# Keys and values of all batches made between two layers, and the fill-in chunks of a turn laid out anew

## What is computed

```python
# layer 0: x += tanh(g)*mix(ctx, norm(x)); x += tanh(g)*moe64(norm(x))    (64 experts, top 8)
# layer 1, attention: 16 heads of 16, causal, keys and values from ctx_512 (4, 256, 64)
qp = norm(x) @ Wq.T
k, v = split(ctx_512 @ Wkv_expand.T)          # do not depend on x
scores = einsum(q, k) / 4, causal mask; attn = softmax(scores)
x = x + tanh(g_xattn[1]) * (attn @ v) @ Wout.T
# layer 1, experts: 8 routed (top 2) + shared (2 more chunks), all computed for all tokens
x1, x3 = silu(xf @ w_gate), xf @ w_up         # 10 chunks of 128 hidden units
x = x + tanh(g_ffn[1]) * sum_c comb_c * (x1*x3)_c @ w_down_c
```

## Time and profile before

| | us |
|---|---|
| median of 3 runs (612.03 to 613.97) | 612.97 |
| the profiled execution's own time | 607.06 |
| span of that execution, first to last instruction | 605.3 |
| PE busy in the span | 425.7 (70%) |
| DVE busy | 346.5 (57%) |
| ACT busy | 184.0 (30%) |
| POOL busy | 146.3 (24%) |
| mean granted TensorE clock | 0.834 of full |

### The profile page before, as it was taken

How to read it: one execution, slowest core, us unless ns; L and a number is a source line. 1 busy time by engine, 2 the same in 40 slices (tenths; PEclk the granted TensorE clock), 3 DMA queues, 4 the chain that set the end, 5 groups by cost and what they waited for, 6 DMA issues and landing times.

```text
span 605.3 us, 9222 instructions
## 1 busy us (share of the span) xinstructions
PE 425.7 (70%) x2738; PEld 355.7 (59%) x2738; DVE 346.5 (57%) x1050; ACT 184.0 (30%) x377; POOL 146.3 (24%) x154
## 2 busy tenths in 40 slices
PE   5065553302999999997136637899699978999686
PEld 3043342202998889885025425787488856887586
DVE  2978875396344444443367803487547883681554
ACT  3212210100333333343611412525252342517231
POOL 1306675673000000002775370001710000000000
PEclk9976565555999999997557756999779996999899
DMA  7996222266699999993332130000310000000000
GB/s 272 427 410 264 88 96 79 78 238 211 209 301 322 324 312 326 377 396 128 100 91 67 38 104 0 1 2 16 100 44 0 2 0 0 18 2 2 2 17 18
DMA packets 36693, 82.96 MB, mean 137 GB/s; under 512 B 6000, under 2 KB 16048, under 8 KB 34864
## 3 DMA queue, kind: packets, MB, share of 16 engines
q1 hardware_dynamic: 22800, 55.83, 26.3%
q0 software_dynamic: 6144, 16.79, 8.6%
q10 hardware_dynamic: 7712, 9.90, 4.6%
HBM read 50.44 MB, written 31.92 MB: 136 GB/s over the span
## 4 chain that ended last, share of the span: by engine, by line
PE 52%; DVE 15%; issue 12%; ACT 7%; POOL 6%; another core or an unknown queue 4%; DMA 2%; SPq 1%; DVEq 0%; POOLq 0%; ACTq 0%
PE PS L555 11%; PE PS L565 7%; POOL slots_in L432 5%; PE PS L644 4%; PE PS L618 4%; PE PS L542 3%; PE PS L764 2%; PE PS L657 2%; PE PS L712 2%; PE PS L659 2%; PE PS L658 2%; DVE TH L1312 2%; DVE WORK L1049 2%; DVE TOP L1045 2%
## 5 line engine op out<-in xcount | busy, mean ns | idle before, releaser
L442 POOL DMA_INDIRECT GB<-slots_out,IDXG x64 | 68.4, 1069 | 214.9 <-SPq L365 139.7
L555 PE MATMUL PS<-XTE,WR 128*128 128x128 f32 (+2 forms) x512 | 79.7, 299 | 0.0
L432 POOL DMA_INDIRECT slots_in<-XNA,IDX x64 | 64.9, 1014 | 36.8 <-issue 27.6
L555 PEld LDWEIGHTS PS<-XTE,WR 128*128 128x128 f32 x512 | 70.2, 193 | 0.6 <-ACT XTE L854 0.4
L1234 DVE TENSOR_TENSOR HE<-SGE,PS 128x128 f32<-128x128 f32 (+2 forms) x64 | 20.0, 312 | 62.9 <-ACT SGE L863 60.0
L565 PE MATMUL PS<-WR,HE 128*80 128x256 f32 (+2 forms) x198 | 53.6, 381 | 0.3 <-DVE HE L1234 0.3
L657 PE MATMUL PS<-XH,WGH 128*128 128x256 f32 x160 | 49.7, 311 | 0.3 <-DVE XL L1430 0.3
L854 ACT COPY XTE<-PS 128x256 f32<-128x256 f32 (+2 forms) x64 | 26.3, 410 | 74.5 <-PE PS L542 70.6
L644 PE MATMUL PS<-WD,XW 128*128 128x256 f32 x160 | 41.8, 384 | 7.0 <-DVE XW L1319 3.5
L542 PE MATMUL PS<-CF,XE 80*128 80x80 f32 (+2 forms) x198 | 28.3, 256 | 25.7 <-DMA XE<-slots_in 25.7
L658 PE MATMUL PS<-XL,WGH 128*128 128x256 f32 x160 | 45.3, 283 | 0.0
(11 more groups left out here) (226 smaller groups left out, 843.2 us busy)
## 6 DMA issues: line engine op xcount, KB each, us to landing
WR<-in_wexp SPq DMA_DIRECT2D x64, 384.0 KB, 5.0
slots_in<-GB SPq DMA_DIRECT2D x12, 1024.0 KB, 18.7
XE<-slots_in SPq DMA_DIRECT2D x24, 160.0 KB, 4.5
slots_out<-OE ACTq DMA_DIRECT2D x24, 160.0 KB, 4.3
XE<-slots_in SPq DMA_DIRECT2D x29, 128.0 KB, 5.2
slots_out<-OE ACTq DMA_DIRECT2D x29, 128.0 KB, 5.1
WGU<-in_wgu SPq DMA_DIRECT2D x1, 2560.0 KB
XE<-slots_in SPq DMA_DIRECT2D x11, 192.0 KB, 4.0
```

Of the source, the lines that this page charges most:

```text
L432: pool.indirect_dma_start(out=xs, out_offset=bass.IndirectOffsetOnAxis(ap=IDX[:, t, j:j + 1], axis=0), in_=XNA[:, t, :], in_offset=None, b ...
L442: pool.indirect_dma_start(out=GB[:, t % BT, j, :], out_offset=None, in_=ys, in_offset=bass.IndirectOffsetOnAxis(ap=IDXG[:, t, j:j + 1], ax ...
L555: last = mm(psGE[place % 2][:, a, 0:cap(place)], W13[:, k, a, :], XTE[:, place % 2, k, 0:cap(place)], start=(k == 0), stop=(k == KC - 1))
```

## The change

The keys and values of all four batches are made in the transition, before turn 0. ACT now also casts the keys' spreading matrices (`SPREADK`) and makes a negated identity `NEG`. For each batch: PE makes keys and values straight from `CT`, ACT copies the rounded keys into `KP[:, 0]` and the values into `VA` or, for batches 1 to 3, `VC`. The remainder is no longer DVE's: PE computes the keys again and adds `NEG` times the rounded part (`keys_rest`), and ACT copies it into `KP[:, 1]`. PE spreads in two halves into banks 4 to 7, ACT takes each half (128x1024), batch 0 into `KS`, the others into a staging buffer that lies in `WGL`'s memory, and issues a DMA of 1 MB to `keys_kept` in device memory. Only then follow the cast of the queries' matrices, the zeroing of `QS` and the rounding of the weights.

In a turn, `keys`, `values`, `spread_keys` and their copies are gone from PE, ACT and DVE. SP loads the next batch's 1 MB of keys into `KS` once the last average of the turn is done, behind the eight DMAs of `maxima_rows` and ahead of the output's store. POOL, behind the gathers, copies the next values from `VC` to `VA` (128x512) and no longer fills `CTB`. Three loads (`wk1`, `wv1`, `spread`, 640 KB together) move from the end of the start's loads to ahead of `x`.

The chunks are laid out anew: 0 behind the `XN` transposes, 1 behind the query projection, 2 behind the spread, 3, 4 and 5 in the stage-one loop after units 1, 3 and 5, 6 behind it, none ahead of stage two. Chunks 7, 8 and 9 are split into their twelve matmuls and the `down`s, which stand singly: `up(7)` behind the last average, `down(6)` behind L752, `up(8)`, `down(7)`, `up(9)` behind the output projection, `down(8)` behind L776, `down(9)` behind the gate. On DVE, chunk 7 moves from ahead of the combining to behind L1417, chunk 8 from ahead of L1413 to behind the norm, chunk 9 behind `XL`.

```diff
 # PE
+            def keys_rest(b):
+                pe.wait_ge(S["k_high"], b + 1)
+                pe.wait_ge(S["k_low"], b)
+                for m in range(KC):
+                    mm(psKl[:, m, :], WK1[:, m, :], CT[:, b * N:(b + 1) * N], start=True, stop=False)
+                    last = mm(psKl[:, m, :], NEG[:, :], KP[:, 0, m, :], start=False, stop=True)
+                last.then_inc(S["k_rest"], 1)
+            def spread_keys(b):
+                pe.wait_ge(S["k_low"], b + 1)
+                for p in range(2):
+                    if b:
+                        pe.wait_ge(S["ks_set"], b * 2 + p - 1)
+                    for g in range(4 * p, 4 * p + 4):
+                        for i in range(2):
+                            last = mm(psKp[:, g, :], SPREADK[:, i, g % (UNITS // KC), :], KP[:, i, g // (UNITS // KC), :],
+                                      start=(i == 0), stop=(i == 1))
+                    last.then_inc(S["k_spread"], 1)
+            pe.wait_ge(S["loaded_kv"], 48)
+            pe.wait_ge(S["spread_set"], 2)
             keys(0)
-            values(0)
-            spread_keys(0)
+            for b in range(B):
+                keys_rest(b)
+                if b + 1 < B:
+                    keys(b + 1)
+                spread_keys(b)
+            pe.wait_ge(S["ks_set"], 2 * B)
+            pe.wait_ge(S["va_set"], B)
             pe.wait_ge(S["e_zeros"], 1)
             turn(0, None, True)
...
 # ACT
-            A.copy(SPREAD[:, :, :, :], SPREADB[:, :, :, :]).then_inc(S["e_spread"], 1)
+            A.copy(SPREADK[:, :, :, :], SPREADB[:, 0:2, :, :]).then_inc(S["spread_set"], 1)
+            A.mul(NEG[:, :], ident, -1.0).then_inc(S["spread_set"], 1)
...
             def spread_keys(b):
-                act.wait_ge(S["e_k_spread"], b + 1)
-                A.activation(KS[:, :, :], psK, ACT.Identity, bias=one_rows).then_inc(S["e_ks"], 1)
+                if b > 2:
+                    act.wait_ge(S["ks_kept0"], 16)
+                for p in range(2):
+                    act.wait_ge(S["k_spread"], b * 2 + p + 1)
+                    half = slice(4 * p, 4 * p + 4)
+                    to = KST[:, (b - 1) % 2, half, :] if b else KS[:, half, :]
+                    A.activation(to, psKp[:, half, :], ACT.Identity, bias=one_rows).then_inc(S["ks_set"], 1)
+                if b:
+                    act.wait_ge(S["ks_set"], (b + 1) * 2)
+                    act.dma_start(kst[b * P:(b + 1) * P, :], ...)
+            keys(0)
+            keys_rest(0)
+            for b in range(B):
+                if b + 1 < B:
+                    act.wait_ge(S["k_spread"], b * 2 + 2)
+                    keys(b + 1)
+                    keys_rest(b + 1)
+                spread_keys(b)
+            A.copy(SPREAD[:, :, :, :], SPREADB[:, 2:4, :, :]).then_inc(S["e_spread"], 1)
...
 # PE, end of a turn
-                fill(8)
+                up(7)
                 pe.wait_ge(S["e_os"], b + 1)
...
-                if ahead:
-                    keys(b + 1)
+                sum_down(6)
...
-                if ahead:
-                    pe.wait_ge(S["e_x3"], b + 1)
-                    values(b + 1)
-                    spread_keys(b + 1)
-                    pe.wait_ge(S["e_va"], b + 2)
-                fill(9)
+                up(8)
+                sum_down(7)
+                up(9)
                 pe.wait_ge(S["e_xn3"], b + 1)
...
 # DVE
             def low_weights(first):
                 dve.wait_ge(S["e_wh"], 1)
+                dve.wait_ge(S["ks_kept0"], 32)
+                dve.wait_ge(S["ks_kept1"], 16)
```

More of the change, by code:

```diff
@@ L444, in gather, with gathers @@
                                             bounds_check=SLOTS_OUT - 1, oob_is_err=False).then_inc(gathered[t % BT][j], 16)
[L447 removed]
+            def gathers(b):
                 for i in range(BT):
@@ L452, in _, with values @@
                     gather(b * BT + i)
-                if b:
-                    pool.wait_ge(S["e_v"], b)
-                    nc.gpsimd.tensor_copy(CTB[:, :], CT[:, b * N:(b + 1) * N]).then_inc(S["e_ctx"], 1)
+            def values(b):
+                pool.wait_ge(S["va_set"], b + 1)
+                pool.wait_ge(S["e_av"], b * HG)
+                nc.gpsimd.tensor_copy(VA[:, :, :, 0:HD], VC[:, b - 1, :].rearrange("p (t h c) -> p t h c", t=BT, h=NH)).then_inc(S["va_in"], 1)
+            gathers(0)
+            gathers(1)
+            for b in range(1, B):
+                if b + 1 < B:
+                    gathers(b + 1)
+                values(b)
         @block.tensor
@@ L612, in _, with spread @@
             pe.wait_ge(S["general_done"], 1)
-            def spread(dst, part, which):
+            def spread(dst, part):
                 for g in range(UNITS):
                     for i in range(2):
-                        last = mm(dst[:, g, :], SPREAD[:, which + i, g % (UNITS // KC), :], part[:, i, g // (UNITS // KC), :],
+                        last = mm(dst[:, g, :], SPREAD[:, i, g % (UNITS // KC), :], part[:, i, g // (UNITS // KC), :],
                                   start=(i == 0), stop=(i == 1))
                 return last
[L622 to L637, removed]
             def down(f, c):
@@ L698, in turn @@
                 last.then_inc(S["e_q"], 1)
+                fill(1)
+                pe.wait_ge(S["e_spread"], 1)
+                pe.wait_ge(S["e_lo_q"], b + 1)
+                spread(psQ, QP).then_inc(S["e_q_spread"], 1)
                 fill(2)
[L701 to L704, removed]
                 pe.wait_ge(S["e_qs"], b * 4 + 4)
+                if f is not None:
+                    pe.wait_ge(S["ks_in"], b * 16)
                 for u in range(UNITS):
@@ L722, in turn @@
                 flip_maxima(b, 1)
-                fill(7)
                 def average(g):
+                    if g == 0 and f is not None:
+                        pe.wait_ge(S["va_in"], b)
                     pe.wait_ge(S["e_exp"], b * NH + (g + 1) * GH)
```

146 lines of the change are left out of this document (85 added, 61 removed).

## The result

The changed kernel takes 646.0 us (median; 642.1 to 646.5), the kernel before 612.5 in the runs beside it (609.4 to 614.0): ratio 1.055, 95% interval 1.049 to 1.060. It is 33 us slower, where 3.5 faster was forecast. The profiled executions have spans of 640.3 and 605.3 us; the four turns begin, by PE's first transpose of each, at 354.9, 431.4, 498.8 and 555.5 us, where they began at 310.7, 383.4, 451.0 and 517.5.

What follows compares the result with a forecast made beforehand. No engine bounds it throughout: the transition waits for gathers, turns 1 and 2 are nearly PE's work plus 9 us of gaps. 12 - 12 - 1.5 - 2 = -3.5 us, from 612.97 to 609.5 us; range 601 to 618.

Steps and rivals of the forecast that it cites:

- the term of +12 for the transition: Between 282 us and turn 0: making all keys and values there delays batch 0's transposes 11.2 us, plus 0.8 for semaphores.
- The stops under the gathers: Transition: ACT's unexplained stops of 3 to 6 us, seen in turn 0, were given no time in the sum.
- the cycle of 6.4 us: Transition: one batch's exchange between PE and ACT, from one spreading's end to the next, at full clock.
- The slower rival: PE's and ACT's exchange over `KP`, 283 to 312: stays cold or stalls, 4.7 us more per cycle, typically 617; chance 0.21.
- The reason given for the full clock: Transition: batch 0's matmuls stand back to back, and PE is busy 5.6 of 6.4 us, as densely as in turns 1 and 2.
- The bound of +26 for the cold case: Transition: if PE stays at 1.2 GHz throughout, a cycle takes 11.0 us and the transition costs 26 us, the upper bound.
- the sum of -6 a turn: Turns 1 and 2: earlier transposes, moved chunks and covered table-load holes win 6 us each, 4 to 9.
- The sign that was to show it: Turns 1 and 2: the transposes of L776 follow DVE's norm within 1 us; today they come 3.56 us late.
- Turn 3 with the rest: Turn 3 gets the same chunk layout, partly given back behind the turn: -2 us, 0 to -4.
- Turn 0: `keys` ahead of L759 and a chunk's matmuls ahead of turn 1's first transposes go: -1.5 us, 0 to -3.
- The start: The start's loads: 640 KB moved ahead of `x` cost 0, at most 0.5 us.
- the kept keys: Key writes to device memory cost 0, or 2 us if the last takes 10; loads back into `KS` cost 0.

Runs made afterwards that it cites:

- e1_hold: The changed kernel with POOL waiting for the last half of the keys before it issues the gathers of batches 0 and 1: 645.1 us, ratio 1.051.
- e8_warm: e1_hold with extra bf16 matmuls of 512 columns ahead of the key chain and within it: a cycle of 9.55 us, total time not given.
- e4_plain: The changed kernel with the gathers of batches 0 and 1 replaced by as many ordinary DMAs from SP: 626.5 us in one execution.
- e16_before_paced: The kernel before with the gathers of batches 2 and 3 given out one at a time on steps of the turns: 590.5 us, ratio 0.964.
- e17_after_paced: The changed kernel with the gathers of batches 2 and 3 given out one at a time on steps of the turns: 623.4 us, ratio 1.016.
- e9_burst: The kernel before with ten PE bursts of 16 fp32r matmuls, each answered by ScalarE, ahead of the transition's work, gathers in flight; total time not given.

## Why the prediction was wrong

Two steps failed, both in the term of +12 for the transition, which measured +44.2. The stops under the gathers were put at nothing in the sum, and cost about 22 us; the cycle of 6.4 us took the full clock, and the chain ran at the lower one, which made it 21.9 us instead of 12.

**The evidence against the stops.** The slower rival named the mechanism's place, ACT's and PE's exchange between 283 and 312, and its sign: the unexplained stops under gathers. It was set aside because none stood in the chain from 282 to 299, "with gathers running too". That inference failed. The kernel before has none there for want of instructions, not for immunity: between the gathers' start and 310 its PE issues 32 loads and matmuls, and when the same kernel is given bursts, trips or copies at this place, it stops. The change adds the very thing that was scarce. The rival allowed for two stops of 3 to 6 us; they were three and cost 20 to 23 us.

**The clock in the chain.** `e1_hold` shows cycles of 9.2 to 11.5 us without stops, `e8_warm` 6.7 at full clock. The reason given for the full clock was that PE is as densely busy as in the turns; it was busy 83% of the time and stayed at 0.54 in the mean, near the lower level. The section of the Trainium skill that the prediction weighed ("TensorE: Matmul & The Clock Gate", "Why this matters for your kernels") speaks of idle gaps between bursts; with the same holes of 0.75 us `e8_warm` has a clock of 1.00, so this case doesn't show that holes so short bring the half rate. The bound of +26 for the cold case was sound: 11.0 a cycle was predicted, 11.5 the longest, and in `e4_plain`, without stops and nearly as cold (0.62), turn 0 begins 21.9 us later than before. The other 22.3 of the 44.2 are the stops. With the cold chain alone the forecast would have been 619, just outside the range; with the stops as well no case of the prediction comes near 646.

**Turns 1 and 2.** Forecast -6 each, measured -0.2 and -9.8. With paced gathers on both sides (`e16_before_paced` to `e17_after_paced`) they are -5.9 and -7.1. So the sum of -6 a turn was right, though its single terms weren't measured; in turn 1 the stops (3.3 + 4.5 + 7.3 us, where before had 4.0) took the gain, and in turn 2 the clock gave more. The sign that was to show it holds there: the second transposes start at 550.6, right behind DVE's norm, which ends at 550.5. Turn 3 with the rest gains 6.5 in this pair and 3.0 in the original one, against 2.

**Turn 0.** Forecast -1.5, measured +3.8, and +4.0 in the paced pair: this term had the wrong sign. The clock is 0.61 there in the paced kernel, where it is 0.82 without the hoist. What keeps it low isn't settled; it follows a transition that ends cold.

**The start, the kept keys.** Forecast 0. The gathers start at 283.6, where they did at 282.9. The last write of keys, issued at 349.8, lands in 3.9 us, before `WGH` ends at 359.1; no wait of PE for the kept keys or values shows. Both steps held.

## What to carry to other kernels

Count instructions, not only microseconds, wherever GpSimd issues indirect transfers one behind the other: here an engine had 80 to 100 to spend, then at most 1.4 per us. Transfers with tens of microseconds of slack should be given out with pauses, tied to steps of the engines that they would starve. A chain of short matmuls between copies can't be costed at full clock only because PE is busy in it; here the cold duration was the right one and the warm one the bound.

## What the runs showed of the hardware

- Under gathers 1.3 us apart PE and ScalarE took 0.70 us or more per instruction after some 80 to 100, in all 132 or 133 in some 45 us, unrolled or (PE) in a loop. As many ordinary DMAs of the same size, within 19 us, held up nothing in one execution. VectorE was only tried with 32 trips.
- The trace shows this under two names: idling put down to "issue" where the engine itself is read, and "remote" or "another core or an unknown queue" where its customer is. The recorded end of a burst lay 23 us ahead of its signal (303.7 and 327.0 in `e9_burst`).
- PE busy 83% of 49 us in the chain of `e1_hold` stood at a mean clock of 0.54; with bf16 matmuls of 512 columns ahead and in between (`e8_warm`) it was 1.00.
